# A second residual that reaches the output by a store and an accumulating transfer from GpSimd

## The chip, the cores and the metric

The kernel runs on one core of a Trainium2 chip. The metric is the device time of one execution in microseconds; lower is better. All data are float32.

## What is computed

Input and output are 4 sequences of 2048 tokens with 256 features. A Mamba layer (`_L0_attn_ref`) and an RWKV channel mixing (`_L0_ffn_ref`) follow each other, each with a residual around it:

```
x = x + mamba(layernorm(x))
x = x + ffn(layernorm(x))

# mamba: x, z = x_in @ W_in; delta, B, C from x
h = dA_t * h + dBx_t                # 256 x 16 states, step by step over the sequence
y_t = sum_n h * C_t
y = (y + x * D_param) * silu(z) @ W_out
res = y + x_in;  return layernorm(res) * ln_g + ln_b

# ffn
xr = mu_r * x + (1 - mu_r) * x_prev;  xk = mu_k * x + (1 - mu_k) * x_prev
r = sigmoid(xr @ W_r.T)
return r * (square(relu(xk @ W_k.T)) @ W_v.T)
```

The change concerns the last addition: the gated value r * v, and the residual x that goes into the sum with it (called the second residual, `xres` in the kernel).

## The kernel before

The tokens are cut into 16 chunks of 512 (`NT`), four to a sequence. Every engine runs a program of its own, written out by hand; semaphores tie the programs together. The main loop has a step for each chunk t. A step has 16 columns n, one for each of the 16 states of the Mamba layer, and ScalarE and VectorE count 32 places in it, two to a column. The tables `ACT_TURN`, `VEC_TURN` and `PE_TURN` say at which place (TensorE: at which column) each other piece of work is slipped in between the columns; `ACT_TAIL`, `VEC_TAIL` and `PE_TAIL` do so for the last step, and `BANK` and `TAIL_BANK` say which of three PSUM banks a product uses. The order in each program is fixed by these tables.

For a column, ScalarE computes exp(delta * A) for both halves of the features into a ring of three banks (`exps`, L654). GpSimd multiplies delta * x by the B row (`times_b`, L542), three columns ahead of the scan, into a ring of four slots (`dbx`). VectorE scans both halves (`scans`, L1033). The product with the C row is made by VectorE for 8 or 9 of the columns of a step (L1040, L1049, the tables `SPLITS`) and for the others by GpSimd, one column behind (`times_c`, L555), after ScalarE has saved the last state as carry (L660, L665). TensorE adds the products up in `y_ps` (`add_up`, L1317), two columns behind. The B and C rows come from DRAM through two-slot rings of four columns (`load_b` L436, `load_c` L445), issued by SyncE.

Between these columns a step t does the work before the scan for chunk t+1, the work behind the scan for chunk t-1 (gating by VectorE L1131, output product, layer norm, the sum of the first residual L1465, ScalarE's copy with sums into `xres`, `nm`, `ln_sum[3]` at place 28, and the norm `norm3` at place 31, which counts `hn_done`), and the channel mixing for chunk t-2. For the latter ScalarE copies the transposed rows (`hT_in`, L709 and L710), VectorE mixes (`mix`, L1086), TensorE computes r, k and v, ScalarE takes tanh of r into `r_out` (`tanh_r`, L723). In `out_of` (L1095) VectorE computes (1 + r) * v from `r_out` and the bank of v and writes it back into the bank, at place 31. TensorE then adds the second residual of chunk t-2 by an identity product into the same bank (the loop over `xo0`, `xo1`, L1479), ScalarE copies the bank to `r_out` (places `ev0`, `ev1`, L889), and SyncE stores `r_out` to the output (L482). `v` and `xo` are in columns 12 and 13 of TensorE's program. `xres` has two halves, one for the chunk being finished and one for the chunk behind it; SyncE loads each with the input of its chunk (L451).

Chunks 0 to 13 go this way. Chunk 14 (`out_late`) and chunk 15 (`close`) have code of their own, in which VectorE adds the residual.

The lines that matter in the old program:

```
for j in range(2):                                                   # TensorE, L1479
    last = pe.matmul(by_block(bank(t, f"v{v}"))[:, j, :], ident[:, :], xres[:, t % 2, 2 * v + j, :],
                     start=False, stop=True, skip_group_check=True)
act.activation(r_out[:, 2 * v:2 * v + 2, :], by_block(bank(t, f"v{v}")),
               ACT.Copy).then_inc(read_sem(t, f"v{v}"), 1)           # ScalarE, L889
sp.dma_start(out_v[c], r_out[:, :, :]).then_inc(s["out_stored"], 16) # SyncE, L482
```

Of the kernel before, what the change touches and what calls it, by code (L numbers as in the profile page):

```python
# [7 lines left out]
NS = 16  # L8
# [6 lines left out]
GN = 4  # L15
# [43 lines left out]
                late_prev=16, square=16, sum30=16, sum3_set=16, sq3=16, rs3=17, norm3=18, ev1=18, late_hT0=19,  # L59
                late_hT1=19, ev0=22, late_k1=24, late_k0=27, late_square=27, late_tanh=31)  # L60
VEC_TAIL = dict(mix1=2, mix0=2, gate=6, x21=15, x20=15, v1=17, v0=18, late_mix1=20, late_mix0=20)
PE_TAIL = dict(hT0=0, hT1=0, r0=2, r1=2, gT0=3, gT1=3, wo0=4, wo1=4, k1=4, k0=5, xD=6, xa0=6, xa1=6, xo1=7, v0=7,
               v1=7, late_hT1=9, xo0=9, late_hT0=9, late_k1=12, late_r0=12, late_k0=12, late_r1=13)
# [32 lines left out]
def mamba_rwkv_layer(nc, x_in, W_in, W_x, W_dt, b_dt, A_log, D_param, W_out, ln_g, ln_b,  # L96
# [12 lines left out]
    with ExitStack() as ctx:  # L109
# [6 lines left out]
        def sem(name):  # L116
            return ctx.enter_context(nc.semaphore(name))
# [83 lines left out]
            x_loaded xres_loaded bc_stored out_stored start_ready  # L201
# [15 lines left out]
        out_ready = [sem(f"out_ready{v}") for v in range(2)]  # L217
# [196 lines left out]
        def _(sp):  # L414
# [33 lines left out]
            def step(t, par, pre=False, scan=False, mid=False, end=False, late=False, more=False):  # L448
                start = t == -1
                if mid:  # L450
                    sp.dma_start(xres[:, 1 - par, :, :], x_v[t - 1]).then_inc(s["xres_loaded"], 16)  # L451
                if scan:
                    if not (t == 0):
                        load_c(t, 1)
# [23 lines left out]
                for mark, c in ended(t, end, late):  # L478
                    if c < LAST - 1:
                        for v in range(2):  # L480
                            need_read(sp, t, f"{mark}v{v}")
                        sp.dma_start(out_v[c], r_out[:, :, :]).then_inc(s["out_stored"], 16)  # L482
                    if late and c == LAST - 2:
                        sp.dma_start(xres[:, LAST % 2, :, :], x_v[LAST]).then_inc(s["xres_loaded"], 16)
                        need(sp, s["dbx_done"], NS * LAST + GN * (GROUPS - 1))
                        sp.dma_start(w_r_raw, halves(W_r)).then_inc(s["w_r_loaded"], 16)
# [11 lines left out]
            sp.wait_ge(s["out_stored"], 16 * (NT + 2))  # L498
# [57 lines left out]

# [24 lines left out]
        def _(act):  # L581
# [85 lines left out]
            def step(t, par, pre=False, scan=False, mid=False, end=False, late=False, more=False):  # L667
# [943 lines left out]
```

## Time and profile before

| | |
|---|---|
| median of 3 runs | 942.68 us (942.14 to 942.72) |
| profiled execution, its own time | 944.42 us |
| its span, first to last instruction | 942.6 us |
| its mean granted TensorE clock | 0.973 |
| VectorE busy | 900.9 us (96%) |
| GpSimd busy | 889.1 us (94%) |
| TensorE busy | 864.2 us (92%) |
| ScalarE busy | 847.9 us (90%) |
| moved by DMA | 163.60 MB, mean 174 GB/s |

The profile is that of one execution. PE is TensorE, PEld its weight loads, DVE VectorE, ACT ScalarE, POOL GpSimd and SP SyncE; a q behind a name is that engine's sequencer, which issues transfers. L with a number is a line of the kernel. A group of instructions is written "out<-in", with partitions x elements. "Idle before" is the time in which the engine had nothing running before an instruction, and the name behind the arrow is what ended it. A transfer that GpSimd issues has a row with a duration on GpSimd itself; the busy share of section 1 does not count it.

### The profile page before, as it was taken

How to read it: one execution, taken by the hardware profiler on the slowest of the kernel's cores; microseconds unless marked ns; L12 is line 12 of the kernel's file. 1: busy time of each engine (PE TensorE's matmuls, PEld its weight loads, DVE VectorE, ACT ScalarE, POOL GpSimd, SP SyncE). 2: the span in 40 equal slices, each digit the busy share in tenths (PEclk: the TensorE clock that was granted, in tenths of full speed). 3: DMA queues.
4: the chain of work that ended last, by engine and by line, in shares of the span. 5: the costliest groups of instructions: out<-in, count | busy, mean ns of one | idle time of the engine just before them, and what ended most of it. 6: DMA issues, size and time to landing. Idle time of an engine off the chain costs nothing.

```text
span 942.6 us, 15838 instructions
## 1 busy us (share of the span) xinstructions
PE 864.2 (92%) x5024; PEld 688.7 (73%) x5024; DVE 900.9 (96%) x985; ACT 847.9 (90%) x2064; POOL 889.1 (94%) x399
## 2 busy tenths in 40 slices
PE   8757679999999899989999899998999999999998
PEld 5545567877878587787868678786778768778876
DVE  4899989999999999999999999999999999999896
ACT  5886988989999999998999999999999999978875
POOL 4999999999999999999999989999999999999970
PEclk9987898999999999999999999999999999999999
DMA  7445435462534644455463644446354354446231
GB/s 222 156 177 204 175 138 204 179 235 104 210 157 161 239 164 172 183 178 166 174 248 147 224 148 160 179 179 248 125 210 179 143 198 179 157 160 223 91 101 45
DMA packets 49938, 163.60 MB, mean 174 GB/s; under 512 B 5248, under 2 KB 33152, under 8 KB 33600
## 3 DMA queue, kind: packets, MB, share of 16 engines
q1 hardware_dynamic: 48528, 161.27, 46.2%
q0 software_dynamic: 512, 1.31, 0.5%
q8 instruction: 40, 0.66, 0.3%
q14 instruction: 42, 0.34, 0.1%
q10 hardware_dynamic: 816, 0.02, 0.1%
HBM read 153.15 MB, written 9.44 MB: 172 GB/s over the span
## 4 chain that ended last, share of the span: by engine, by line
PE 46%; ACT 28%; DVE 15%; issue 9%; DMA 1%; POOL 0%; POOLq 0%; DVEq 0%; SPq 0%; ACTq 0%
PE w_ps L1326 10%; ACT da_ps L654 10%; PE y_ps L1317 9%; PE w_ps L1350 6%; DVE da_ps L1033 5%; PE w_ps L1359 4%; PE w_ps L1362 4%; DVE hg L1049 3%; DVE hg L1033 3%; PE w_ps L1465 3%; DVE hg L1040 2%; PE w_ps L1368 2%; ACT xn_tok L591 2%; ACT h_tok L591 2%; ACT zs L715 2%
## 5 line engine op out<-in xcount | busy, mean ns | idle before, releaser
L542 POOL TENSOR_TENSOR dbx<-u,b_ring 128x1024 f32<-128x1024 f32 x255 | 599.4, 2380 | 4.7 <-DVE hg L1033 4.6
L654 ACT ACTIVATE da_ps<-delta,a_neg 128x512 f32<-128x512 f32 x512 | 340.0, 684 | 23.9 <-DVE hg L1040 7.3
L555 POOL TENSOR_TENSOR hg<-hg,c_ring 128x1024 f32<-128x1024 f32 x122 | 290.4, 2381 | 8.5 <-ACT carry L660 6.7
L1317 PE MATMUL y_ps<-ident,hg 128*128 128x128 f32 x2048 | 264.3, 279 | 9.2 <-POOL hg L555 9.0
L1317 PEld LDWEIGHTS y_ps<-ident,hg 128*128 128x128 f32 x2048 | 241.7, 145 | 35.9 <-issue 17.8
L1033 DVE TENSOR_TENSOR_SCAN da_ps<-da_ps,carry,dbx 128x512 f32<-128x512 f32 x203 | 249.8, 1271 | 4.3 <-ACT da_ps L654 4.1
L1033 DVE TENSOR_TENSOR_SCAN hg<-da_ps,carry,dbx 128x512 f32<-128x512 f32 x181 | 220.3, 1263 | 1.4 <-ACT carry L660 1.2
L1040 DVE TENSOR_TENSOR hg<-da_ps,c_ring 128x1024 f32<-128x1024 f32 x68 | 82.3, 1210 | 0.2
L1049 DVE TENSOR_TENSOR hg<-da_ps,c_ring 128x512 f32<-128x512 f32 x130 | 82.3, 673 | 0.0
L1033 DVE TENSOR_TENSOR_SCAN da_ps<-da_ps,dbx 128x512 f32<-128x512 f32 x64 | 75.8, 1213 | 3.3 <-ACT da_ps L654 2.8
L1326 PE MATMUL w_ps<-xnT_ring,w_in 128*128 128x512 f32 x120 | 61.4, 636 | 16.0 <-ACT xT L696 14.1
L1033 DVE TENSOR_TENSOR_SCAN hg<-da_ps,dbx 128x512 f32<-128x512 f32 x64 | 74.6, 1206 | 1.6 <-ACT da_ps L654 1.6
L1359 PE MATMUL w_ps<-w_rT,mixed 128*128 128x256 f32 x240 | 61.8, 380 | 0.3 <-DVE mixed L1086 0.3
L1362 PE MATMUL w_ps<-w_r_prev,mixed 128*128 128x256 f32 x240 | 61.6, 379 | 0.0
L1350 PE MATMUL w_ps<-w_in,xnT_ring 128*128 128x256 f32 x248 | 59.3, 382 | 0.6 <-ACT delta L688 0.3
L1326 PE MATMUL w_ps<-xnT_ring,w_dtx 128*128 128x512 f32 x120 | 57.9, 606 | 0.9 <-ACT bc_rows L800 0.9
L1350 PE MATMUL w_ps<-w_out,gated 128*128 128x256 f32 x248 | 58.7, 379 | 0.0
L1326 PE MATMUL w_ps<-mixed,w_kT 128*128 128x512 f32 x120 | 58.0, 607 | 0.1
L1350 PEld LDWEIGHTS w_ps<-w_in,xnT_ring 128*128 128x128 f32 x248 | 45.5, 190 | 14.5 <-ACT kact L682 4.8
L1359 PEld LDWEIGHTS w_ps<-w_rT,mixed 128*128 128x128 f32 x240 | 44.4, 190 | 12.0 <-issue 6.7
L1350 PE MATMUL w_ps<-w_vT,kact 128*128 128x256 f32 x232 | 52.6, 379 | 0.0
L1362 PEld LDWEIGHTS w_ps<-w_r_prev,mixed 128*128 128x128 f32 x240 | 45.6, 190 | 6.2
(212 smaller groups left out, 1333.0 us busy)
## 6 DMA issues: line engine op xcount, KB each, us to landing
c_ring<-bc_rows_dram SPq DMA_DIRECT2D x64, 1024.0 KB, 4.7
b_ring<-bc_rows_dram SPq DMA_DIRECT2D x63, 1024.0 KB, 6.7
xres<-in_L_attn_x_in_dram SPq DMA_DIRECT2D x16, 512.0 KB, 4.8
x_tok<-in_L_attn_x_in_dram SPq DMA_DIRECT2D x15, 512.0 KB, 5.9
out_dram<-r_out SPq DMA_DIRECT2D x14, 512.0 KB, 3.2
bc_rows_dram<-bc_rows SPq DMA_DIRECT2D x64, 16.0 KB, 5.4
w_in<-in_L_attn_W_in_dram SPq DMA_DIRECT2D x2, 256.0 KB, 4.3
x_tok<-in_L_attn_x_in_dram SPq DMA_DIRECT2D x2, 256.0 KB, 4.6
```

Of the source, the lines that this page charges most:

```text
L542: pool.tensor_tensor(dbx[:, n % X_RING, :, :], u[:, ip, :, :], b.to_broadcast([P, KH, LC]), ALU.mult).then_inc(s["dbx_done"], 1)
L555: pool.tensor_tensor(part, part, c_of(n).to_broadcast([P, KH, LC]), ALU.mult).then_inc(s["g_pool"], 1)
L591: last = act.activation(dst[j], src[j], ACT.Identity, scale=rs[j], bias=nm[j])
L654: act.activation(da_of(n, h), delta[:, ip, h, :], ACT.Exp, scale=a_neg[:, h, n:n + 1]).then_inc(s["da_ready"], 1)
L1033: dve.tensor_tensor_scan(out, da_of(n, h), dbx[:, n % X_RING, h, :], 0.0 if first else carry[:, n, h:h + 1], ALU.mult, ALU.add).then_inc(s ...
L1040: dve.tensor_tensor(hg[:, n % H_RING, :, :], da_both(n), c_of(n).to_broadcast([P, KH, LC]), ALU.mult).then_inc(s["g_vec"], 1)
L1049: last = dve.tensor_tensor(hg[:, n % H_RING, h:h + 1, :], da_ps[:, at:at + 1, :], c_of(n), ALU.mult)
L1317: last = pe.matmul(y_tok[:, b, h * P:(h + 1) * P], hg[:, n % H_RING, h, b * P:(b + 1) * P], ident[:, :], is_transpose=True, start=n == 0 a ...
L1326: last = pe.matmul(out, w[:, k, cols], x[:, k, :], start=k == 0, stop=k == KH - 1)
L1350: last = pe.matmul(by_block(out)[:, b, :], xT_[:, k, tokens], w[:, k, :], start=b == 0 and k == 0 and not begun, stop=k == KH - 1, skip_gr ...
L1359: pe.matmul(by_block(out)[:, b, :], h_of[:, k, at_b + 1:at_b + 1 + P], w_rT[:, k, :], start=k == 0, stop=False)
L1362: last = pe.matmul(by_block(out)[:, b, :], h_of[:, k, at_b:at_b + P], w_r_prev[:, k, :], start=False, stop=k == KH - 1)
```

## The change

The sum is made in the output instead of in the bank. In step t SyncE stores the second residual of chunk t-2 from `xres` to the output as soon as its mean exists (`ln_sum[3]`). VectorE's `out_of` writes (1 + r) * v to `r_out` and not to the bank. In step t+1, at GpSimd's column `OUT_TURN` = 2 (in the last step also at `OUT_TAIL` = 12), GpSimd issues a transfer of `r_out` to the output that adds to what stands there (`add_out`). TensorE's `xo0` and `xo1` and ScalarE's `ev0` and `ev1` are gone. The load of `xres` now waits for that store (`x2_stored`) and for the norm that reads the same half (`hn_done`), and `tanh_r` waits for the accumulating transfer (`out_added`) before it writes `r_out` again. Chunks 14 and 15 stay as they were.

```diff
-                sum30=25, sum31=27, sum3_set=28, sq3=28, rs3=29, ev0=31, ev1=31, norm3=31)
+                sum30=25, sum31=27, sum3_set=28, sq3=28, rs3=29, norm3=31)
-               x1=6, wo1=7, wo0=7, k1=7, xa1=9, xa0=9, xD=10, v0=12, v1=12, xo0=13, xo1=13)
+               x1=6, wo1=7, wo0=7, k1=7, xa1=9, xa0=9, xD=10, v0=12, v1=12)
+OUT_TURN, OUT_TAIL = 2, 12
...
                 if mid:
+                    need(sp, s["x2_stored"], 16 * (t - 2))
+                    need(sp, s["hn_done"], t - 2)
                     sp.dma_start(xres[:, 1 - par, :, :], x_v[t - 1]).then_inc(s["xres_loaded"], 16)
+                if end:
+                    need(sp, ln_sum[3], t - 1)
+                    sp.dma_start(out_v[t - 2], xres[:, par, :, :]).then_inc(s["x2_stored"], 16)
...
-                for mark, c in ended(t, end, late):
-                    if c < LAST - 1:
-                        for v in range(2):
-                            need_read(sp, t, f"{mark}v{v}")
-                        sp.dma_start(out_v[c], r_out[:, :, :]).then_inc(s["out_stored"], 16)
...
+            def add_out(t, c):
+
+                for v in range(2):
+                    need_read(pool, t, f"v{v}")
+                need(pool, s["x2_stored"], 16 * (c + 1))
+                pool.dma_start(out_v[c], r_out[:, :, :], accum_op=ALU.add).then_inc(s["out_added"], 16)
+
...
                 for n in range(NS):
+                    if t >= 3 and n == OUT_TURN:
+                        add_out(t - 1, t - 3)
+                    if late and n == OUT_TAIL:
+                        add_out(t, t - 2)
...
-                        need(act, s["out_stored"], 16 * c)
+                        need(act, s["out_added"], 16 * c)
...
-                    for v in range(2):
-                        if end and at(f"ev{v}"):
-                            need(act, out_ready[v], t - 1)
-                            act.activation(r_out[:, 2 * v:2 * v + 2, :], by_block(bank(t, f"v{v}")),
-                                           ACT.Copy).then_inc(read_sem(t, f"v{v}"), 1)
...
-                    dve.scalar_tensor_tensor(b, part, 1.0, b, ALU.add, ALU.mult).then_inc(s[f"gv{v}_done"], 1)
+                    dve.scalar_tensor_tensor(part, part, 1.0, b, ALU.add, ALU.mult).then_inc(read_sem(t, f"v{v}"), 1)
...
-                    for v in range(2):
-                        if end and n == turn[f"xo{v}"]:
-                            need(pe, s[f"gv{v}_done"], t - 1)
-                            need(pe, ln_sum[3], t - 1)
-                            for j in range(2):
-                                last = pe.matmul(by_block(bank(t, f"v{v}"))[:, j, :], ident[:, :], xres[:, t % 2, 2 * v + j, :],
-                                                 start=False, stop=True, skip_group_check=True)
-                            last.then_inc(out_ready[v], 1)
```

How the orders move. First GpSimd's program in the middle of the kernel, from the end of one step over columns 1 to 7 of the next; `dbx` rows are products with B, `hg` rows products with C. Before:

```order
L542 TENSOR_TENSOR dbx<-u,b_ring 128x1024 x3
L555 TENSOR_TENSOR hg<-hg,c_ring 128x1024
L542 TENSOR_TENSOR dbx<-u,b_ring 128x1024 x2
L555 TENSOR_TENSOR hg<-hg,c_ring 128x1024
L542 TENSOR_TENSOR dbx<-u,b_ring 128x1024 x2
L555 TENSOR_TENSOR hg<-hg,c_ring 128x1024
```

The same piece of GpSimd's program in the changed kernel, where the lines of the file have shifted by three:

```order
L545 TENSOR_TENSOR dbx<-u,b_ring 128x1024 x3
L558 TENSOR_TENSOR hg<-hg,c_ring 128x1024
L545 TENSOR_TENSOR dbx<-u,b_ring 128x1024 x2
L558 TENSOR_TENSOR hg<-hg,c_ring 128x1024
L545 TENSOR_TENSOR dbx<-u,b_ring 128x1024
L565 DMA out_dram<-r_out 128x4x256
L545 TENSOR_TENSOR dbx<-u,b_ring 128x1024
L558 TENSOR_TENSOR hg<-hg,c_ring 128x1024
```

The accumulating transfer (L565) has come between the products of columns 4 and 5 with B; nothing else in GpSimd's program has moved.

Second, SyncE's program at the turn from one step to the next. Before:

```order
L445 DMA c_ring<-bc_rows_dram 128x2048
L436 DMA b_ring<-bc_rows_dram 128x2048
L482 DMA out_dram<-r_out 128x4x256
L451 DMA xres<-in_L_attn_x_in_dram 128x4x256
L445 DMA c_ring<-bc_rows_dram 128x2048
L457 DMA x_tok<-in_L_attn_x_in_dram 128x4x256
```

SyncE's program at the same place in the changed kernel:

```order
L445 DMA c_ring<-bc_rows_dram 128x2048
L436 DMA b_ring<-bc_rows_dram 128x2048
L453 DMA xres<-in_L_attn_x_in_dram 128x4x256
L456 DMA out_dram<-xres 128x4x256
L445 DMA c_ring<-bc_rows_dram 128x2048
L462 DMA x_tok<-in_L_attn_x_in_dram 128x4x256
```

The store has another source and stands behind the load of `xres`, no longer ahead of it.

## Rows read from the trace of the kernel before

**Rows 1.** The page: busy us of each engine, share of the span, instructions.
```profile
PE 864.2 (92%) x5024; PEld 688.7 (73%) x5024; DVE 900.9 (96%) x985; ACT 847.9 (90%) x2064; POOL 889.1 (94%) x399
```

**Rows 2.** Stretch 193:873: us; busy PE, PEld, DVE, ACT, POOL; PEclk, DMA share, GB/s.
```profile
193.00:873.00 680.00, 646.90 (x3828) 519.75 (x3827) 672.17 (x702) 643.18 (x1579) 669.11 (x288) 0.99 0.49 182
```

**Rows 3.** VectorE's gating: duration min/median/max in ns, first and last start.
```profile
L1131 DVE TENSOR_TENSOR gated_tok<-y_ps,zs x15: 1195/1196/1199, 93.6 to 870.1; 128x1024 f32<-128x1024 f32 x15
```

**Rows 4.** VectorE's waits, 195 to 873 us: in total, times, longest.
```profile
DVE mixed L1086 <- ACT mixed L710: 2.6, 5, 0.6
DVE da_ps L1033 <- ACT da_ps L654: 1.7, 6, 0.3
DVE hg L1033 <- ACT carry L660: 1.2, 1, 1.2
DVE w_ps L1095 <- PE w_ps L1350: 0.6, 3, 0.2
```

**Rows 5.** GpSimd's waits, 195 to 916 us.
```profile
POOL hg L555 <- ACT carry L660: 5.8, 6, 1.7
POOL dbx L542 <- DVE hg L1033: 4.6, 6, 1.3
POOL hg L555 <- DVE hg L1033: 1.4, 1, 1.4
POOL hg L555 <- issue: 0.3, 1, 0.3
```

**Rows 6.** TensorE's timeline at the end of a step: start, us, instruction.
```profile
357.80 1.89 PE L1479 MATMUL w_ps<-xres,ident 128*128 128x256 f32 x8
359.53 2.78 PE L1317 MATMUL y_ps<-ident,hg 128*128 128x128 f32 x24
```

**Rows 7.** Groups by line: busy us, mean ns of one | idle before, releaser.
```profile
L1078 DVE SCALAR_TENSOR_TENSOR zs<-zs,w_ps 128x512 f32<-128x512 f32 x31 | 20.8, 672 | 1.0 <-ACT zs L715 1.0
L1095 DVE SCALAR_TENSOR_TENSOR w_ps<-r_out,w_ps 128x512 f32<-128x512 f32 x28 | 18.1, 680 | 2.9 <-PE w_ps L1350 2.9
L889 ACT ACTIVATE r_out<-w_ps 128x512 f32<-128x512 f32 x28 | 14.9, 579 | 0.0
```

**Rows 8.** SyncE's timeline at the turn of a step.
```profile
360.84 0.39 SPq L482 DMA_DIRECT2D out_dram<-r_out  x1
...
364.41 0.33 SPq L445 DMA_DIRECT2D c_ring<-bc_rows_dram  x1
```

**Rows 9.** GpSimd's timeline at the start: nothing in it waits.
```profile
2.62 1.23 POOL L512 TENSOR_SCALAR_AFFINE_SELECT pick<-pick 128x512 f32<-128x512 f32 x2 [0.21 <-POOL pick L508]
3.79 0.90 POOL L515 DMA_DIRECT2D h_tok<-in_L_ffn_W_r_dram  x1
4.68 0.73 POOL L516 DMA_DIRECT2D h_tok<-in_L_ffn_W_k_dram  x1
5.41 0.72 POOL L518 DMA_DIRECT2D mur<-in_L_ffn_mu_r_dram  x1
...
8.29 0.57 POOL L522 DMA_DIRECT2D g_all<-in_L_attn_ln_g_dram  x1
```

**Rows 10.** GpSimd's timeline: two of the thirteen gaps from 195 to 900 us.
```profile
219.67 2.36 POOL L542 TENSOR_TENSOR dbx<-u,b_ring 128x1024 f32<-128x1024 f32 x1 [1.30 <-DVE hg L1033]
...
341.05 2.36 POOL L555 TENSOR_TENSOR hg<-hg,c_ring 128x1024 f32<-128x1024 f32 x1 [1.71 <-ACT carry L660]
```

**Rows 11.** Timeline of the last step's end, GpSimd, then TensorE.
```profile
909.55 4.71 POOL L555 TENSOR_TENSOR hg<-hg,c_ring 128x1024 f32<-128x1024 f32 x2 [1.40 <-DVE hg L1033]
914.21 1.27 POOL L576 TENSOR_TENSOR hg<-hg,c_ring 128x512 f32<-128x512 f32 x1
915.63 1.06 PE L1317 MATMUL y_ps<-ident,hg 128*128 128x128 f32 x8 [0.20 <-POOL hg L576]
```

**Rows 12.** DMA issues: KB each, median us from issue to landing.
```profile
b_ring<-bc_rows_dram SPq DMA_DIRECT2D x63, 1024.0 KB, 6.7
out_dram<-r_out SPq DMA_DIRECT2D x14, 512.0 KB, 3.2
```

More of the change, by code:

```diff
@@ L58 @@
 ACT_TAIL = dict(prev=0, hT1=2, hT0=2, tanh=8, gT1=9, gT0=9, k1=11, sq20=12, sq21=13, rs2=14, k0=15, sum31=16,
[L59 to L60 removed]
+                late_prev=16, square=16, sum30=16, sum3_set=16, sq3=16, rs3=17, norm3=18, late_hT0=19,
+                late_hT1=19, late_k1=24, late_k0=27, late_square=27, late_tanh=31)
 VEC_TAIL = dict(mix1=2, mix0=2, gate=6, x21=15, x20=15, v1=17, v0=18, late_mix1=20, late_mix0=20)
[L62 to L63 removed]
+PE_TAIL = dict(hT0=0, hT1=0, r0=2, r1=2, gT0=3, gT1=3, wo0=4, wo1=4, k1=4, k0=5, xD=6, xa0=6, xa1=6, v0=7,
+               v1=7, late_hT1=9, late_hT0=9, late_k1=12, late_r0=12, late_k0=12, late_r1=13)
 TAIL_BANK = dict(v1=2, v0=1, late_r1=1, hT0=0, k1=2, late_hT1=0, gT1=1, r0=1, hT1=1, r1=0, late_k0=0, k0=0,
@@ L200, in mamba_rwkv_layer @@
             a_exped a_set omu_set setup_pe setup_ev
-            x_loaded xres_loaded bc_stored out_stored start_ready
+            x_loaded xres_loaded bc_stored x2_stored out_added out_stored start_ready
             xn_done bc_rows_done
@@ L216, in mamba_rwkv_layer @@
         ln2_g = [sem(f"ln2_g{v}") for v in range(2)]
-        out_ready = [sem(f"out_ready{v}") for v in range(2)]
         ln_nr = {ln: sem(f"ln{ln}_nr") for ln in nm}
@@ L477, in step @@
                         load_c(0, 1, True)
-                for mark, c in ended(t, end, late):
-                    if c < LAST - 1:
-                        for v in range(2):
-                            need_read(sp, t, f"{mark}v{v}")
-                        sp.dma_start(out_v[c], r_out[:, :, :]).then_inc(s["out_stored"], 16)
[L483 to L486, printed above, removed]
+                if late:
+                    need(sp, s["x2_stored"], 16 * (LAST - 1))
+                    need(sp, s["hn_done"], LAST - 1)
+                    sp.dma_start(xres[:, LAST % 2, :, :], x_v[LAST]).then_inc(s["xres_loaded"], 16)
+                    need(sp, s["dbx_done"], NS * LAST + GN * (GROUPS - 1))
+                    sp.dma_start(w_r_raw, halves(W_r)).then_inc(s["w_r_loaded"], 16)
             def close():
@@ L497, in _ @@
             steps(sp, step, close)
-            sp.wait_ge(s["out_stored"], 16 * (NT + 2))
+            sp.wait_ge(s["out_added"], 16 * (NT - 2))
+            sp.wait_ge(s["out_stored"], 16 * 4)
         @block.gpsimd
@@ L957, in close @@
                 share(1, xr, omr, KH)
-                act.wait_ge(s["out_stored"], 16 * (NT - 2))
+                act.wait_ge(s["out_added"], 16 * (NT - 2))
                 tanh(0)
@@ L1163, in out_late @@
                     dve.scalar_tensor_tensor(b, part, 1.0, b, ALU.add, ALU.mult).then_inc(s[f"gv{v}_done"], 1)
-                    need(dve, s[f"gv{v}_done"], LAST)
+                    dve.wait_ge(s[f"gv{v}_done"], 1)
                     need(dve, ln_sum[3], LAST)
```

## The prediction

> **What bounds the kernel now.** I read the busy shares first. The reader is to see that four engines stand above 90% of the 942.6 us span, VectorE highest at 96% [rows 1]. A share of the whole span does not say which of them is the bound, so I then read the busy time of the stretch from 193 to 873 us, twelve chunks of the steady part [rows 2]. There VectorE works 672.2 of 680 us (7.8 us idle), GpSimd 669.1 (10.9 us idle), TensorE 646.9 (33 us idle), ScalarE 643.2 (37 us idle). The time from one gating of VectorE to the same one a chunk later is (870.1 - 93.6) / 14 = 55.5 us [rows 3]. So the kernel goes at VectorE's pace, and GpSimd is 0.9 us per chunk behind it in load: two engines are the bound, and the two that the change relieves are not among them. The third view is the waits. From 195 to 873 us the four largest of VectorE's waits make 6.1 us, 2.6 of them for ScalarE's copy of the transposed rows, 1.7 for its exponentials, 1.2 for a carry, 0.6 for TensorE [rows 4]. GpSimd's own waits from 195 to 916 us add up to 12.1 us [rows 5]: 5.8 for saved carries, 4.6 and 1.4 for a scan, 0.3 for nothing shown. These 12.1 us are all the room that GpSimd has.
>
> **Taken from TensorE.** Eight rows of L1479 per chunk go, in fourteen chunks. In the timeline eight of them start at 357.80 and the next group at 359.53, so 1.73 us per chunk, 24.2 us in all [rows 6]. TensorE had 33 us idle in the steady part and more will be idle now. Nobody waits there for it: VectorE's 0.6 us is all. Worth nothing directly. Two waits of TensorE go with it: the one for VectorE's gated value at column 13 and the one for the sum of the residual; neither shows as idle time.
>
> **Taken from ScalarE.** Two copies of 579 ns per chunk, 28 in all, 16.2 us [rows 7]. ScalarE's norm of the next chunk stands four places behind them and gets about 1.1 us earlier, and so does the copy for which VectorE waits. At best VectorE's 2.6 us for that copy goes. The exponentials wait for VectorE's scans through three banks, so a lighter ScalarE does not start them earlier. Gain between 0 and 2.6 us, and only while VectorE is the bound.
>
> **VectorE** keeps its instruction, which now writes SBUF in place of the bank. The row of the present one is 680 ns, and a row of the same operation with a bank in and SBUF out has 672 ns [rows 7]: 28 x 8 ns = 0.2 us, taken as nothing.
>
> **SyncE.** One transfer per chunk stays one transfer of the same size: the residual goes out where the result went out. It now stands behind the load of the residual, with a wait for the mean of chunk t-1, set at place 28, where the old one waited for the copy at place 31. The old store was issued at 360.84, and the next load of C rows at 364.41, only when GpSimd had read the ring [rows 8]. The new wait ends earlier and that load is still held by GpSimd, so nothing behind it moves. The load of the residual gets two waits, for the store of the step before and for the norm of chunk t-3; both are a chunk old by then. Nothing.
>
> **Added to GpSimd: the term that decides.** One accumulating transfer per chunk, 13 of them between the products of columns 4 and 5 in steps 3 to 15 and a fourteenth in the last step, is written out by GpSimd's own instruction, in order with its products. The old trace has no accumulating transfer and no transfer of 512 rows from GpSimd. Its nearest rows are the nine at the start, of which four stand here [rows 9]: transfers of 128 rows take 0.55 to 0.57 us, those of 256 rows 0.72 us whatever a row holds (1 KB in the weights, 4 bytes in the small vectors). 128 rows more cost 0.16 us (0.72 less 0.56); 512 rows give an estimate of 0.72 + 2 x 0.16 = 1.04 us. The first of them, right behind a compute instruction, took 0.90 and not 0.73 us, 0.17 more. In the steady part each stands behind a compute instruction. I take 1.21 us. The lower end is 0.72 (the number of rows stops mattering), the upper 1.85 (below). Its two waits cost nothing: the two products of VectorE stand before the chunk's end, and GpSimd gets to this place only behind a scan of the next chunk; the residual was stored a chunk before.
>
> **The sum.** 14 x 1.21 = 16.9 us more work on GpSimd, against 12.1 us of waits that it can fill. I went through the thirteen gaps before the tail in order of time: the one of 1.3 us at 219 us comes when only one transfer was added and leaves 0.1 unused, and one of 1.7 us at 341 us leaves 0.2 [rows 10]; all later ones are used up. GpSimd ends 16.9 - 11.8 = 5.1 us late, at some 920.6 us in place of 915.5. Up to there VectorE hardly feels it: GpSimd works three columns of 55.5 / 16 = 3.5 us ahead of the scans, 10.4 us less 2.4 for its own product [rows 11], so it has 8 us. Then it does: GpSimd's two last products started at 909.55 after the 1.4 us wait, the last half product at 914.21, and TensorE waited for it [rows 11]. Behind that stands the chain of the last chunk, untouched by the change. So +5.1 us on the profiled execution, 944.42 us: 949.5. The median of the runs, 942.68, is 1.7 us below that execution; on its scale I forecast **947.8 us**.
>
> **Rival 1: GpSimd's work fits, faster.** If a transfer costs no more than 12.1 / 14 = 0.86 us, GpSimd stays inside its waits and VectorE sets the pace, without some of its waits for ScalarE. At 0.72 us, 10.1 us go into 12.1, and VectorE's 2.6 us [rows 4] are the gain: 940.1. For it: 256 rows take no longer whether they hold 1 KB or 4 bytes. Against it: 128 rows take 0.16 less, so rows do count. The Trainium skill (DMA: Bandwidth & Descriptors, Anatomy of one DMA) says that many descriptors can be emitted before their added cost shows; the 0.16 us that this trace adds between 128 and 256 rows already speaks against that. Chance 0.17, with no change if the cost lies between 0.7 and 0.95 (0.13 of its own, 942.7).
>
> **Rival 2: the addition doubles what has to be read.** An adding transfer must read the output as well as the tile. If the part of GpSimd's work that grows with rows goes by reads, there are 1024: 0.72 + 6 x 0.16 = 1.68, and 0.17 behind a compute instruction, 1.85 us. 14 x 1.85 = 25.9, less 12.1: +13.8 us, 956.5. By then GpSimd is more than 8 us late and VectorE's scans wait for its products from about step 12. For it: nothing in the rows. Against it: nothing either; a plain transfer reads once per row. The Trainium skill (Collectives: The Full Stack, The bandwidth ceiling) states that a reducing transfer has two read descriptors per chunk against one of a copy; no run here shows that for this kind. Chance 0.20.
>
> **Rival 3: the transfer itself disturbs the ring loads.** It reads and writes the output, 0.5 MB each way beside a DMA share of 0.49 [rows 2], where a plain store of that size landed in 3.2 us and B loads in 6.7 [rows 12]. A ring slot is refilled four columns, 13.9 us, before its next use, so a load may be 7 us late before anyone waits. A transfer that took the engines for 10 us would cost some 3 us per chunk, 42 us: 985. Nothing waits for a load in the steady part now. Chance 0.04.
>
> TensorE's clock was granted at 0.99 from 193 to 873 us, nearly all at the upper level, 2.4 GHz [rows 2]. Should its longer waits bring it down now and then, it has 2.7 us free per chunk now (33 / 12.3) and 4.4 after the change, so this changes no number.
>
> **How the numbers follow.** Forecast (transfer of 0.95 to 1.5 us, +1.2 to +9 us) 0.46; rival 2 0.20; rival 3 0.04; rival 1 0.17; no change 0.13. What this kernel's measurement can tell from no change is 0.2%, 1.9 us. Faster: 0.15 (rival 1 without its smallest gains). Same: 0.02 of rival 1, 0.13 and 0.04 of the forecast's lower end, 0.19. Slower 0.66. The range goes from rival 1's 940.1 to 957, which takes in rival 2.
>
> **What the profile of the changed kernel would show.** The row of the accumulating transfer on GpSimd, 14 times, near 1.2 us: below 0.9 is rival 1, above 1.6 rival 2. GpSimd's waits from 195 us on down from 12.1 to under 1.5 us, its last half product near 919 us, TensorE waiting for it. VectorE busy as before, its waits for ScalarE's copy gone and in their place some for GpSimd's product near the end. L1479 and L889 gone. B and C loads landing within 1 us of 6.7 and 4.7. I am wrong if GpSimd still waits for carries all through, or if VectorE waits for loads.

## The result and the profile after

| | before | changed |
|---|---|---|
| median of four executions | 942.70 us | 953.84 us (951.74 to 957.35) |
| ratio to before, 95% interval | 1 | 1.0123 (1.0088 to 1.0158) |
| profiled execution, its span | 942.6 us | 949.9 us |
| mean granted TensorE clock of that execution | 0.973 | 0.960 |
| first gating of VectorE to the last | 93.6 to 870.1 (776.5 us) | 93.2 to 872.4 (779.2 us) |
| last gating to the end of the span | 72.5 us | 77.5 us |

The change costs 11 us by the medians. The profiled execution is the shortest of the four: the two of them with a clock of 0.960 took 951.7 and 952.2 us, the two with 0.955 took 955.5 and 957.4. Its own difference is 7.3 us: 0.4 less up to the first gating, 2.7 more in the steady part, 5.0 more behind the last gating.

Changed kernel, the page's line of busy times, against [rows 1]:

```profile
PE 847.6 (89%) x4912; PEld 676.5 (71%) x4912; DVE 901.1 (95%) x985; ACT 834.8 (88%) x2036; POOL 903.7 (95%) x413
```

GpSimd has 14 instructions and 14.6 us more (these are the transfers; its busy time does count them, other than I wrote ahead of the rows), VectorE the same, TensorE 16.6 and ScalarE 13.1 us less. TensorE should have lost 24.2 us for its 112 rows; that it lost less means that its other rows got longer. The table by stretches has the reason in its clock column. It stands against [rows 2] (us; busy PE, PEld, DVE, ACT, POOL; PEclk, DMA share, GB/s):

```profile
193.00:873.00 680.00, 626.46 (x3668) 504.99 (x3669) 667.55 (x697) 627.45 (x1546) 675.60 (x299) 0.97 0.56 188
```

The granted clock fell from 0.99 to 0.97, and VectorE's idle time rose from 7.8 to 12.5 us (680 less 667.55). The gating, against [rows 3]:

```profile
L1140 DVE TENSOR_TENSOR gated_tok<-y_ps,zs x15: 1197/1199/1200, 93.2 to 872.4; 128x1024 f32<-128x1024 f32 x15
```

What VectorE waits for, 195 to 873 us, against [rows 4] (us in total, times, longest):

```profile
DVE mixed L1095 <- ACT mixed L724: 6.3, 10, 1.2
DVE da_ps L1042 <- ACT da_ps L668: 3.9, 8, 0.8
```

The wait for ScalarE's copy of the transposed rows was to go; it went from 2.6 to 6.3 us. GpSimd's waits, 195 to 925 us, against [rows 5]:

```profile
POOL hg L558 <- ACT carry L674: 3.7, 4, 1.7
POOL hg L558 <- DVE hg L1042: 1.4, 1, 1.4
POOL dbx L545 <- DVE hg L1042: 0.6, 2, 0.3
```

They fell from 12.1 to 5.7 us, not to under 1.5: GpSimd filled its room, and a slower VectorE gave it new room. And TensorE's largest wait, 195 to 925 us, in the kernel before and in the changed one:

```profile
PE w_ps L1368 <- ACT xn_tok L591: 24.7, 12, 2.1
```

```profile
PE w_ps L1377 <- ACT xn_tok L605: 45.1, 12, 3.9
```

**What the transfer costs on GpSimd.** GpSimd's timeline of the changed kernel (start, us, instruction; in square brackets the idle time before it and what ended it):

```profile
756.46 3.35 POOL L545 TENSOR_TENSOR dbx<-u,b_ring 128x1024 f32<-128x1024 f32 x1
758.76 2.31 POOL L565 DMA_DIRECT2D out_dram<-r_out  x1
759.57 3.90 POOL L545 TENSOR_TENSOR dbx<-u,b_ring 128x1024 f32<-128x1024 f32 x1
```

The rows overlap here: the transfer starts at 758.76, while the product ahead of it ends at 759.81. So a row's own length is no cost. From end to end the transfer took 1.26 us (761.07 less 759.81). Over all fourteen this sum is 16.55 us, 1.18 us each (from 0.74 for the first to 1.27), and the product behind the transfer still takes 2.4 us from end to end (763.47 less 761.07).

**Where TensorE's clock falls.** TensorE of the changed kernel at the end of a step:

```profile
421.23 1.56 PE L1377 MATMUL w_ps<-ident,xn_tok 128*128 128x128 f32 x8 [3.65 <-ACT xn_tok L605]
422.58 1.92 PE L1326 MATMUL y_ps<-ident,hg 128*128 128x128 f32 x8
424.29 0.98 PE L1377 MATMUL w_ps<-ident,h_tok 128*128 128x128 f32 x4
```

The same place in the kernel before:

```profile
421.35 1.06 PE L1368 MATMUL w_ps<-ident,xn_tok 128*128 128x128 f32 x8 [2.00 <-ACT xn_tok L591]
422.26 1.04 PE L1317 MATMUL y_ps<-ident,hg 128*128 128x128 f32 x8
```

The transposes start at the same time within 0.12 us, so ScalarE's norm did not get earlier. TensorE waits 1.65 us longer, near the 1.73 us of the removed products, and then the eight transposes take 1.56 us and not 1.06, and the eight products behind them 1.92 and not 1.04. The stretches of the changed kernel show the clock (columns as above):

```profile
420.00:422.00 2.00, 0.77 (x6) 0.80 (x7) 2.00 (x3) 2.00 (x5) 2.00 (x2) 0.91 0.00 0
422.00:424.00 2.00, 2.00 (x11) 2.00 (x10) 2.00 (x4) 2.00 (x5) 2.00 (x3) 0.50 1.00 381
```

And before, for the second of them:

```profile
422.00:424.00 2.00, 1.38 (x13) 1.14 (x12) 2.00 (x5) 2.00 (x5) 2.00 (x2) 1.00 1.01 385
```

0.50 is the lower level, 1.2 GHz. The Trainium skill (TensorE: Matmul & The Clock Gate, What's actually happening) has these two levels and nothing between them, and says that the clock is throttled unless activity releases it; the 0.50 and the 1.00 agree. The transposes that come next are late, ScalarE's copy of them too, and VectorE's mixing behind it. ScalarE, then VectorE of the changed kernel:

```profile
425.37 0.69 ACT L723 ACTIVATE mixed<-w_ps,omk 128x512 f32<-128x512 f32 x1 [1.08 <-PE w_ps L1377]
```

```profile
426.58 0.75 DVE L1095 SCALAR_TENSOR_TENSOR mixed<-w_ps,muk,mixed 128x512 f32<-128x512 f32 x1 [0.51 <-ACT mixed L724]
```

Of the twelve steps in the steady part, eight of the changed kernel have their xn transposes at 1.5 us or more for eight (1.06 at the upper level), and four of the kernel before. In two more steps of the changed kernel the clock falls as well, but only behind the transposes, as in the stretch behind those at 365.73 us, which still took 1.06 (the other is at 814 to 816 us, with 0.55):

```profile
367.00:369.00 2.00, 2.00 (x11) 1.46 (x8) 2.00 (x3) 1.97 (x6) 2.00 (x2) 0.51 0.96 304
```

So the clock fell in ten steps of twelve, and before in four.

**Why the norm did not get earlier.** The two copies are gone from ScalarE, but a carry behind a product of VectorE stands there, and it now waits. ScalarE of the changed kernel:

```profile
361.47 0.17 ACT L679 ACTIVATE carry<-da_ps 128x2 f32<-128x2 f32 x1 [0.86 <-DVE hg L1058]
```

**The last step.** The tables put the tanh of r at place 8 there (`ACT_TAIL`), against 19 in the others, and it may not write `r_out` before the transfer issued at column 2 has landed. GpSimd, ScalarE and VectorE of the changed kernel, in three answers:

```profile
872.79 1.92 POOL L565 DMA_DIRECT2D out_dram<-r_out  x1
...
916.79 4.71 POOL L558 TENSOR_TENSOR hg<-hg,c_ring 128x1024 f32<-128x1024 f32 x2 [1.36 <-DVE hg L1042]
921.46 1.27 POOL L590 TENSOR_TENSOR hg<-hg,c_ring 128x512 f32<-128x512 f32 x1
```

```profile
879.48 1.08 ACT L737 ACTIVATE r_out<-w_ps 128x512 f32<-128x512 f32 x2 [5.00 <-DMA out_dram<-r_out]
```

```profile
877.13 1.29 DVE L1042 TENSOR_TENSOR_SCAN da_ps<-da_ps,carry,dbx 128x512 f32<-128x512 f32 x1 [1.20 <-POOL dbx L545]
882.61 1.29 DVE L1042 TENSOR_TENSOR_SCAN da_ps<-da_ps,carry,dbx 128x512 f32<-128x512 f32 x1 [4.19 <-ACT da_ps L668]
```

ScalarE waits 5.0 us for the landing, the exponentials are queued behind it, and VectorE waits 4.2 us for them. GpSimd's last half product ends at 922.7 us (915.5 before).

**Landings**, from the page's part on DMA issues (KB each, median us):

```profile
b_ring<-bc_rows_dram SPq DMA_DIRECT2D x63, 1024.0 KB, 6.9
xres<-in_L_attn_x_in_dram SPq DMA_DIRECT2D x16, 512.0 KB, 7.2
...
out_dram<-xres SPq DMA_DIRECT2D x14, 512.0 KB, 8.1
out_dram<-r_out POOLq DMA_DIRECT2D x14, 512.0 KB, 10.9
```

So there are three candidates: GpSimd's added 16.6 us, TensorE's clock, and the wait of the last step. The runs take them apart. Ratios are to the kernel before, timed beside each run.

### The profile page after: what moved, and what is told of

Same layout as the page of the kernel before. It is cut to its first block, busy times and chain, and to the rows that moved or that the text cites. A ratio compares the mean times of both kernels' runs of the same rounds, so it can differ in the third digit from the quotient of the medians.

```text
span 949.9 us, 15587 instructions
## 1 busy us (share of the span) xinstructions
PE 847.6 (89%) x4912; PEld 676.5 (71%) x4912; DVE 901.1 (95%) x985; ACT 834.8 (88%) x2036; POOL 903.7 (95%) x413
## 4 chain that ended last, share of the span: by engine, by line
PE 39%; ACT 29%; DVE 17%; issue 10%; POOL 2%; DMA 1%; DVEq 0%; POOLq 0%; SPq 0%; ACTq 0%
ACT da_ps L668 10%; PE y_ps L1326 9%; PE w_ps L1335 8%; DVE da_ps L1042 6%; PE w_ps L1359 5%; DVE hg L1049 4%; DVE hg L1042 3%; PE w_ps L1368 3%; PE w_ps L1371 3%; PE w_ps L1377 3%; DVE hg L1058 2%; ACT xn_tok L605 2%; PE w_ps L1474 2%; ACT h_tok L605 2%; ACT L822 1%
## 5 line engine op out<-in xcount | busy, mean ns | idle before, releaser
L545 POOL TENSOR_TENSOR dbx<-u,b_ring 128x1024 f32<-128x1024 f32 x255 | 651.3, 2753 | 0.7 <-DVE hg L1042 0.6
L558 POOL TENSOR_TENSOR hg<-hg,c_ring 128x1024 f32<-128x1024 f32 x122 | 334.1, 2738 | 5.1 <-ACT carry L674 3.7
L1377 PE MATMUL w_ps<-ident,xn_tok 128*128 128x128 f32 x120 | 22.0, 344 | 48.9 <-ACT xn_tok L605 48.9
L1377 PEld LDWEIGHTS w_ps<-ident,xn_tok 128*128 128x128 f32 x120 | 17.7, 176 | 52.5 <-issue 52.5
## 6 DMA issues: line engine op xcount, KB each, us to landing
out_dram<-r_out POOLq DMA_DIRECT2D x14, 512.0 KB, 10.9
```

What stands on the lines that cost most here:

```text
L545: pool.tensor_tensor(dbx[:, n % X_RING, :, :], u[:, ip, :, :], b.to_broadcast([P, KH, LC]), ALU.mult).then_inc(s["dbx_done"], 1)
L558: pool.tensor_tensor(part, part, c_of(n).to_broadcast([P, KH, LC]), ALU.mult).then_inc(s["g_pool"], 1)
L1377: last = pe.transpose(bank[:, j * P:(j + 1) * P], src[:, j, k * P:(k + 1) * P], ident[:, :])
```

## The experiments

### The wait of the last step: `tail_early`

```diff
-                    if t >= 3 and n == OUT_TURN:
+                    if t >= 3 and n == (1 if late else OUT_TURN):
```

> The changed kernel with the first transfer of the last step issued at GpSimd's column 1 and not 2. That is two products, 4.6 us, earlier. If the last step's wait of the tanh for the transfer (5.0 us on ScalarE, 4.2 us on VectorE behind it) is what costs there, the wait falls to about 0.5 us and the time by about 4 us against the changed kernel, to some 947.5 for the quickest executions, and the spread between executions (951.7 to 957.4) shrinks. If GpSimd's own load sets the end, as forecast, GpSimd does the same work and the time stays at 952 to 957.

Measured: 956.62 us, 1.0139 (1.0123 to 1.0156), no faster than the changed kernel. The transfer was issued one column sooner, at 872.65 us (872.79 in the changed kernel: in this execution the last gating stands 4.5 us later), and landed 11.7 us later instead of 6.7. The loads of C and B rows were issued at 873.02 and 873.40, right beside it, where in the changed kernel they went out at 868.91 and 869.29; that this is why it landed late is likely, but not shown. The wait became longer, not shorter:

```profile
884.34 1.09 ACT L737 ACTIVATE r_out<-w_ps 128x512 f32<-128x512 f32 x2 [5.29 <-DMA out_dram<-r_out]
```

So moving the issue does not take the wait away, and this run does not price it. Another buffer does, further below. The run also shows what the slower half of the changed kernel's executions looks like, since only the last step differs: at a clock of 0.954 its gatings span 783.7 us, 7.2 more than before, and the time behind them is 77.9 us, 5.4 more.

### The removal alone: `removal_only`

All of the removal and none of the addition: TensorE's and ScalarE's work is gone, VectorE writes `r_out`, SyncE stores it, nothing is stored from `xres`, and GpSimd issues nothing. It leaves out the second residual of chunks 0 to 13.

```diff
-                sum30=25, sum31=27, sum3_set=28, sq3=28, rs3=29, ev0=31, ev1=31, norm3=31)
+                sum30=25, sum31=27, sum3_set=28, sq3=28, rs3=29, norm3=31)
-               x1=6, wo1=7, wo0=7, k1=7, xa1=9, xa0=9, xD=10, v0=12, v1=12, xo0=13, xo1=13)
+               x1=6, wo1=7, wo0=7, k1=7, xa1=9, xa0=9, xD=10, v0=12, v1=12)
...
-                        for v in range(2):
-                            need_read(sp, t, f"{mark}v{v}")
-                        sp.dma_start(out_v[c], r_out[:, :, :]).then_inc(s["out_stored"], 16)
...
+                    for v in range(2):
+                        need_read(sp, t, f"v{v}")
+                    sp.dma_start(out_v[t - 2], r_out[:, :, :]).then_inc(s["out_added"], 16)
```

> Only the removal: TensorE and ScalarE no longer add the second residual, SyncE stores the gated value, GpSimd issues nothing; the second residual is left out of the output of chunks 0 to 13. By the forecast (GpSimd's added load is the only cost) the time is 940 to 942.7. By the rival that TensorE's longer idle time before the transposes of the norm lowers its granted clock and delays VectorE, it is 1 to 3 us slower than before, 943.5 to 945.5, with that idle time at 3.7 us per chunk, the clock near 0.97 from 193 to 873 us, and VectorE's wait for ScalarE's mixed copy near 6 us.

Measured: 952.35 us, **1.0095 (1.0076 to 1.0114)**. Taking work away and adding none costs 9 us, far outside both expectations; the one that named the clock had 1 to 3. VectorE's gating ran from 93.2 to 877.1 us, 783.9 against 776.5; behind it stand 73.2 us against 72.5, so the loss is in the steady part. The stretch, VectorE's largest wait and one of TensorE's rows:

```profile
193.00:873.00 680.00, 627.95 (x3671) 505.98 (x3670) 664.96 (x695) 627.15 (x1544) 660.38 (x285) 0.96 0.48 178
```

```profile
DVE mixed L1088 <- ACT mixed L717: 7.8, 10, 1.2
```

```profile
366.25 1.94 PE L1370 MATMUL w_ps<-ident,xn_tok 128*128 128x128 f32 x8 [3.86 <-ACT xn_tok L598]
```

The clock is at 0.96, GpSimd is busy for 660.4 us only, and nine of twelve steps have slow transposes (in two more the clock falls behind them). GpSimd's waits from 195 us on are 20.1 us, 8 more than before; the two largest:

```profile
POOL hg L555 <- ACT carry L667: 10.7, 10, 1.9
POOL dbx L542 <- DVE hg L1035: 8.2, 6, 1.7
```

The rule that engines off the bound are worth nothing fails in the other direction: less work there made the bound slower.

### Something useless in the place of what was removed: `pe_filled`

The changed kernel, and at column 13 four products of 128x256, as long as the removed ones, into a bank that is free there, in all steps but the last.

```diff
+                    if end and not late and n == 13:
+                        need_read(pe, t, "k1")
+                        for j in range(4):
+                            pe.matmul(by_block(work[0])[:, j % 2, :], ident[:, :], w_in[:, 0, 0:D], start=True, stop=True)
```

> The changed kernel with eight rows of products without use (identity times a weight, into a free bank, result never read) in place of the eight rows that added the residual, in all steps but the last. If TensorE's clock carries the loss of the steady part, TensorE idles 2.1 us per chunk again, the clock is 0.99 there, VectorE's wait for the mixed copy goes back from 6.3 to under 3 us, and the time falls by 2 to 3 us against the changed kernel. If GpSimd's load carries it, nothing changes but TensorE's busy time.

Measured: 949.57 us, 1.0062 (1.0047 to 1.0077): 4 to 6 us faster than the changed kernel by products whose result nobody reads. TensorE's wait for the norm is back at 24.5 us, 2.1 at most, as before, no transposes above 1.46 us, and the clock at 0.99:

```profile
193.00:873.00 680.00, 643.62 (x3807) 514.68 (x3805) 671.17 (x702) 631.28 (x1551) 680.00 (x301) 0.99 0.56 190
```

GpSimd is busy for the whole 680 us: now it is the bound, as forecast. VectorE's gatings start 1.6 us later and span 775.1 us, no longer than before, and the time behind the last of them is 77.5 us against 72.5: what is left of the cost shows mostly at the end, as the forecast had it. The wait of the last step (4.2 us on VectorE) stayed. One expectation failed: VectorE's wait for the copy is not under 3 us:

```profile
DVE mixed L1095 <- ACT mixed L724: 4.5, 5, 2.0
```

The longest of the five ends at 759.37 us, behind one of the three steps in which the clock still falls (0.51 from 756 to 758 us).

### The transfer alone: `transfer_only`

The kernel before in full, and at the same fourteen places of GpSimd's program an accumulating transfer of the same size, from a tile of constants to a scratch tensor, which SyncE fills once. No engine but GpSimd waits for them before the end of the kernel.

```diff
+            def extra_add(c):
+                need(pool, s["w_z_loaded"], 32)
+                need(pool, s["w_r_in"], 16 + 16 * c)
+                pool.dma_start(extra_v[0], extra[:, :, :], accum_op=ALU.add).then_inc(s["w_r_in"], 16)
...
                 for n in range(NS):
+                    if t >= 3 and n == 2:
+                        extra_add(t - 3)
+                    if late and n == 12:
+                        extra_add(t - 2)
```

> The kernel before, whole, with 14 added accumulating transfers of the same size and shape at the same places of GpSimd's program, from a constant tile to a scratch tensor that nobody waits for. This is GpSimd's added load and the added traffic alone. By the forecast about +4.5 us, 947. If GpSimd has more room than its waits show (it may run ahead of what VectorE needs), under +2 us. The transfer should cost 1.2 us of GpSimd's time, counted from end to end.

Measured: 948.54 us, **1.0059 (1.0040 to 1.0077)**, 5.6 us by the ratio and 4.8 by the medians, where the prediction's sum has 5.1. GpSimd's waits from 195 us on are one of 0.4 us; its last half product starts at 917.88 and ends at 919.2 us. VectorE's gatings span 776.2 us, as before (776.5), and 76.1 us follow them against 72.5. In order: GpSimd's waits, then its timeline:

```profile
POOL hg L563 <- ACT carry L677: 0.4, 1, 0.4
```

```profile
753.36 4.04 POOL L550 TENSOR_TENSOR dbx<-u,b_ring 128x1024 f32<-128x1024 f32 x1
755.67 2.99 POOL L568 DMA_DIRECT2D extra_dram<-g_all  x1
```

End to end 1.26 us again (758.66 less 757.40); all fourteen 17.45 us, 1.25 each.

### The same transfer without the addition: `plain_only`

```diff
-                pool.dma_start(extra_v[0], extra[:, :, :], accum_op=ALU.add).then_inc(s["w_r_in"], 16)
+                pool.dma_start(extra_v[0], extra[:, :, :]).then_inc(s["w_r_in"], 16)
```

> As the run with the transfer alone, but the 14 transfers of GpSimd overwrite and don't add. If the addition costs GpSimd something (the second rival), each takes under 1.1 us from end to end, where the adding ones took 1.25, and the time falls by over 2 us from 948.5. If only the 512 rows count, both stay: 1.2 to 1.3 us, 947 to 949. The landing should be quicker than the adding one's.

Measured: 945.80 us, 1.0013 (0.9999 to 1.0028), 3 to 4 us less than with the addition. GpSimd's timeline:

```profile
751.48 2.35 POOL L550 TENSOR_TENSOR dbx<-u,b_ring 128x1024 f32<-128x1024 f32 x1
753.78 0.80 POOL L568 DMA_DIRECT2D extra_dram<-g_all  x1
754.60 2.37 POOL L550 TENSOR_TENSOR dbx<-u,b_ring 128x1024 f32<-128x1024 f32 x1
```

Here rows hardly overlap, and the transfer takes 0.66 to 0.76 us end to end, 10.31 us for all (0.74 each). So 512 rows cost what 256 did (0.72, [rows 9]), and the addition costs 0.5 us.

From start to start both kinds take 0.8 us (0.81 at 758.76 in the changed kernel, 0.82 here), so the row starts do not show the addition, and a balance over the whole run has to decide. From 195 us on, GpSimd's waits fell by 11.7 us in `transfer_only` and its last half product ended 3.7 us later (919.2 against 915.5): 15.4 us, 1.10 a transfer. In `plain_only` the waits fell by 9.4 us (12.1 to 2.7) and that end came 0.3 us earlier (915.2): 9.1 us, 0.65. The two differ by 0.45 us, so the price of the addition stands, and the sums by row ends are if anything a little high.

The landing was expected to be quicker without the addition, and it is, but by little. The plain transfer, then the adding one of `transfer_only`:

```profile
extra_dram<-g_all POOLq DMA_DIRECT2D x14, 512.0 KB, 9.0
```

```profile
extra_dram<-g_all POOLq DMA_DIRECT2D x14, 512.0 KB, 10.9
```

My 1.21 us was the right size from the wrong cause: the growth by rows that I extrapolated is not there, nor are the 0.17 us behind a compute instruction, and part of rival 2, which gave the addition a price, is. The Trainium skill (DMA: Bandwidth & Descriptors, Anatomy of one DMA) says that many descriptors can be emitted before their added cost shows; 0.72 and 0.74 agree, and the prediction was wrong to let the step from 128 to 256 rows speak against it.

### Removal with the clock kept: `removal_filled`

`removal_only`, and eight products of 128x256 right ahead of the wait for the norm.

```diff
+                    if unit == "xnT0" and 2 <= t <= NT - 2:
+                        for j in range(8):
+                            pe.matmul(by_block(out)[:, j % 2, :], ident[:, :], w_in[:, 0, 0:D], start=True, stop=True)
```

> The removal alone (second residual left out of chunks 0 to 13), with eight products without use, 3.5 us, right ahead of TensorE's wait for the norm, where it idles 3.85 us per chunk. If the clock is the whole of the removal's 8.6 us, the transposes behind the wait take 1.06 us in every chunk and no more 1.94, VectorE's wait for the mixed copy falls from 7.8 to under 2 us, and the time is 940 to 943. If something else of the removal costs (another order of ScalarE, VectorE's write to SBUF), the time stays above 948.

Measured: 940.90 us, **0.9968 (0.9955 to 0.9980)**, 12 us less than without them. TensorE:

```profile
358.99 3.62 PE L1390 MATMUL w_ps<-w_in,ident 128*128 128x256 f32 x16
...
362.92 1.09 PE L1370 MATMUL w_ps<-ident,xn_tok 128*128 128x128 f32 x8 [0.31 <-ACT xn_tok L598]
```

```profile
193.00:873.00 680.00, 664.39 (x3912) 530.47 (x3911) 672.03 (x701) 633.95 (x1555) 672.51 (x290) 1.00 0.49 181
```

The useless rows fill 3.6 us of the 3.9 in which TensorE waited anyway, the clock stays at 1.00, and VectorE's wait for the copy falls from 7.8 to 0.3 us. So 12 us hang on the clock. That this run is 3 us faster than the kernel before does not mean that the removal gains 3 us: the kernel before has slow steps of its own, which the next run takes away.

### The same in the kernel before: `before_filled`

Its TensorE waited 2.0 to 2.1 us at this place and had four steps with slow transposes, so it too should gain. On the kernel before:

```diff
+                    if unit == "xnT0" and 2 <= t <= NT - 2:
+                        for j in range(4):
+                            pe.matmul(by_block(out)[:, j % 2, :], ident[:, :], w_in[:, 0, 0:D], start=True, stop=True)
```

> The kernel before with four products without use, 1.73 us, right ahead of the same wait, where it idles 2.1 us per chunk. By the clock theory the remaining slow transposes (5 of 12 chunks) go, with up to 2.6 us of VectorE's waits: 940 to 941.5. If the clock is not what VectorE waits for, 942.7 or more.

Measured: 939.32 us, **0.9957 (0.9945 to 0.9970)**, faster than both kernels. TensorE:

```profile
361.83 1.89 PE L1388 MATMUL w_ps<-w_in,ident 128*128 128x256 f32 x8
...
364.04 1.09 PE L1368 MATMUL w_ps<-ident,xn_tok 128*128 128x128 f32 x8 [0.32 <-ACT xn_tok L591]
```

The steady clock is 1.00, VectorE waits 0.3 us for the copy (2.6 in [rows 4]), and no transposes are slow. It is not slower than `removal_filled` (940.90 us, 0.9968; the intervals overlap): with the clock kept in both, the removal makes no difference that the runs can tell, and its 9 us are the clock's.

### Another buffer for the last step: `tail_tile`

In the changed kernel chunk 13's tanh, gated value and transfer use `xn_tok`, which is free by then; so the tanh does not wait for a landing.

```diff
+        def gated_out(c):
+            return xn_tok if c == LAST - 2 else r_out
...
-                pool.dma_start(out_v[c], r_out[:, :, :], accum_op=ALU.add).then_inc(s["out_added"], 16)
+                pool.dma_start(out_v[c], gated_out(c)[:, :, :], accum_op=ALU.add).then_inc(s["out_added"], 16)
...
-                    to = x_tok if mark else r_out
-                    if not mark:
+                    to = x_tok if mark else gated_out(c)
+                    if not mark and c != LAST - 2:
...
-                    part = r_out[:, 2 * v:2 * v + 2, :]
+                    part = gated_out(t - 2)[:, 2 * v:2 * v + 2, :]
```

> The changed kernel; in the last step tanh, gated value and transfer of chunk 13 use a free tile (xn_tok), so that the tanh waits for no transfer. If that wait (5 us on ScalarE, 4.2 on VectorE) were alone in the last step, the time would fall by 4 us. But GpSimd idled only 1.4 us behind it in the quick execution (2.2 in a slow one), so I expect 1.5 to 2.5 us less than the changed kernel in the same condition, with VectorE then waiting for GpSimd's products, and no idle GpSimd before its last half product.

Measured: 953.37 us, 1.0101 (1.0079 to 1.0124); the interval overlaps that of the changed kernel. In its profile the time behind the last gating is 75.8 us, against 77.5 in the changed kernel and 72.5 in the kernel before. The 5.0 us did not go to VectorE in full, because TensorE was next in line:

```profile
871.11 1.41 PE L1329 MATMUL y_ps<-ident,hg 128*128 128x128 f32 x8 [3.14 <-POOL hg L561]
```

It waits for GpSimd's product, the tanh waits 2.85 us for TensorE, and VectorE still waits 2.8. `transfer_only` has the same wait of TensorE, 2.89 us. So behind the landing stands GpSimd's lateness: of the 5 us of the last step the landing is worth 1.7 in this profile, less than the medians resolve (I had expected 1.5 to 2.5).

### Both repairs: `after_filled` and `after_best`

`after_filled` is the changed kernel with the eight products ahead of the norm's wait, `after_best` the same with the tile of `tail_tile` (its edit is shown in part).

```diff
+                        for j in range(8):
+                            pe.matmul(by_block(out)[:, j % 2, :], ident[:, :], w_in[:, 0, 0:D], start=True, stop=True)
...
-                pool.dma_start(out_v[c], r_out[:, :, :], accum_op=ALU.add).then_inc(s["out_added"], 16)
+                pool.dma_start(out_v[c], gated_out(c)[:, :, :], accum_op=ALU.add).then_inc(s["out_added"], 16)
```

> The changed kernel, whole, with eight products without use ahead of TensorE's wait for the norm. The clock's part goes (the removal alone fell from 952.4 to 940.9 with it); GpSimd's added work stays. With VectorE at its own pace again, GpSimd has no idle time left but before its last products, and the transfer alone took 4.8 us more than before: I expect 945 to 948, the last step's wait for the transfer still there. If the two causes simply added up, it would be 953.8 less 11.5, 942.

> The same with the free tile for chunk 13 in the last step, so that the tanh waits for no transfer. GpSimd sets the end: 1 to 2 us less than with the products alone, 944 to 946, still behind the kernel before with four such products (939.3), since all that the change takes from TensorE and ScalarE is nobody's wait.

Measured: 947.47 us, 1.0045 (1.0031 to 1.0059), and 947.78 us, 1.0045 (1.0031 to 1.0059). The clock gives back 6 to 7 us. The tile adds nothing that the medians show, where I had expected 944 to 946 us, though the two profiled spans differ by 1.4 us. In `after_best` GpSimd has no wait left at all from 195 us on: it is the bound.

### What the runs say together

| ratio to before | as it is | products ahead of the norm's wait |
|---|---|---|
| kernel before | 1 | 0.9957 |
| removal alone | 1.0095 | 0.9968 |
| changed kernel | 1.0123 | 1.0045 |

Read by rows, the lower clock costs 0.4%, 1.3% and 0.8%. Read by columns, the removal costs 1.0% as it is and 0.1% with the clock kept, which the intervals do not tell from nothing; the transfer on top of it costs 0.3% and 0.8%. They hide each other: time in which VectorE waits behind slow transposes is time in which GpSimd catches up (its waits are 20.1 us in `removal_only`, 5.7 in the changed kernel and 1.2 in `after_filled`). So removal (+9.0 us) and transfer (+5.6) are 14.6 us alone and 11 to 12 together.

## Why the prediction was right, and where it was wrong

The sign, and the time within the range: 953.84 us lies in 940.1 to 957.0, 6 us above the forecast. The mechanism of the forecast exists at its forecast size, but a second and larger one was left out. That the range holds the time is partly luck: its upper part was there for rival 2, whose price did not come, and the clock filled it.

- **What bounds the kernel** was read rightly. With the clock kept GpSimd is busy for all 680 us of the stretch (`pe_filled`).
- **The term for GpSimd, 16.9 us against 12.1 us of waits, +5.1 us.** Right: 16.55 us in the changed kernel, and +5.6 us (4.8 by the medians) when it is the only change. Its end was forecast at 920.6 us; alone it was 919.2, in the changed kernel 922.7.
- **The 1.21 us inside that term.** Right in size (1.18 by row ends, 1.10 by the balance of `transfer_only`), wrong in its working: 0.74 for a transfer of 512 rows and 0.5 for the addition. Two errors met, which is luck.
- **"Taken from TensorE ... worth nothing directly", and "this changes no number" of its clock.** This is the step that failed. I had TensorE's idle time per chunk (2.7, then 4.4 us), but as a mean. In the trace most of it is one wait, 2.0 to 2.1 us, some 4 us behind the removed products. It became 3.7 to 3.9, the clock fell in ten steps of twelve where it had in four, and what comes out of TensorE next is on the way to VectorE. Alone that costs 9 us. The question that I put, who waits for the removed products, was answered rightly (nobody: with the clock kept the removal makes no measurable difference) and was the wrong one.
- **"ScalarE's norm of the next chunk ... gets about 1.1 us earlier".** Wrong: the transposes behind it start within 0.12 us of where they did. The carry ahead of it waits for a product of VectorE, which did not move. Had the norm come 1.1 us earlier, TensorE's wait would have grown by only some 0.6 us (1.73 less 1.1, an estimate).
- **"Its two waits cost nothing."** True of GpSimd's waits. The change adds a third, the tanh's wait for the landing, and I had not gone through it for the last step, where the tanh stands eleven places earlier. It shows 5.0 us on ScalarE and 4.2 on VectorE; taking it out gave 1.7 us in one profile, because GpSimd's lateness stands behind it.
- **SyncE and VectorE at nothing.** No experiment is at odds with it, and none tests it by itself. B and C loads landed within 0.2 us of before (6.9 and 4.8). The store landed in 8.1 us against 3.2 [rows 12] and the load of `xres` in 7.2 against 4.8, and no wait for either shows in the views.
- **The signs.** GpSimd's waits under 1.5 us: 5.7 in the changed kernel, 0.4 with the transfer alone. VectorE's wait for the copy gone: it grew to 6.3 us and was the sign of the missing step.
- **The rivals.** Rival 1's price is that of a plain transfer (0.74 us), and then it made no measurable change. Rival 2's mechanism is real with 0.5 us and not 0.64. Rival 3's did not occur in the steady part; in the last step of `tail_early` it may have been the reverse, a transfer held up by ring loads.

What stays open: why the clock falls in one step and not in another with the same wait to 0.25 us, and with it why the executions of the changed kernel split into 0.960 and 0.955; and what sets the landing of an accumulating transfer, which went from 6.7 to 13.8 us within the changed kernel. Whether the 0.5 us are the reads of the output was not taken apart. The Trainium skill (Collectives: The Full Stack, The bandwidth ceiling) gives the reducing transfers of a collective two read descriptors per chunk against one for a copy; that would fit the direction, and no run here shows it.

## What to carry to other kernels

Before work is taken from an engine that nobody waits for, look at the next wait behind it: on TensorE, a wait that grows by the removed time can bring the clock down for the work after it, and that work may be what the bound waits for. Where such a wait is there anyway, useless products right ahead of it cost nothing and gave 0.4% here. A new wait is to be followed through every table that orders its step, the last step's above all, and costs of GpSimd's transfers are to be read from the end of one row to the end of the next, and held against the waits that they filled and the later end. Where a repair is measured on one kernel, measure it on the other too: `removal_filled` alone would have made the removal look like a gain of 3 us.

## What the runs showed of the hardware that was not expected

- Removing 1.73 us of products per chunk ahead of a wait of 2 us made the kernel 0.95% slower (0.96 granted clock against 0.99); a wait of 2.0 to 2.1 us was already followed by slow transposes in four steps of twelve (in `transfer_only`, `plain_only` and `pe_filled`, with the same wait, in one, three and none), and one of 0.3 us in none.
- Issuing an accumulating transfer of 512 rows cost GpSimd 1.18 to 1.25 us by row ends (1.10 by the balance), a plain one 0.74 (0.65), and one of 256 rows 0.72.
- Its landing took 10.9 us in the median where a plain store of that size by SyncE took 3.2 [rows 12]. Most of that is not the addition: a plain transfer from GpSimd at the same places, to a scratch tensor, took 9.0 (`plain_only`). One issued beside two loads of 1 MB took 11.7, one issued 3.5 us behind them 6.7.
- Rows of GpSimd's products beside an accumulating transfer read up to 4.6 us (`transfer_only`), since they overlap; from end to end they still take 2.3 to 2.4.
